# First mixture feed-forward of a two-layer decoder: the gate's exponential on GpSimd, the pads of the third value tile inside the second attention, four down products in a row

## The chip, the cores and the metric

One core of a Trainium2 chip runs the whole program; the other cores are idle. The metric is the device time of one execution in microseconds (us). Three executions of the kernel before give the times below, and a further one was recorded by the profiler. The engines are TensorE (PE, matmuls; "PEld" is its weight load), VectorE (DVE), ScalarE (ACT), GpSimd (POOL) and SyncE (SP), which issues most DMAs here. Each engine works through its own list of instructions in order and waits on semaphores for the others.

## The reference

Eight sequences of 128 tokens with 128 features pass through two decoder layers. Every sublayer is followed by `layernorm(x + sublayer(x))`. The order is self-attention, cross-attention to a context of 77 tokens, mixture feed-forward, then in the second layer a routed attention/state-space block, masked cross-attention and a second mixture. What matters here is the mixture of the first layer, which follows the first cross-attention:

```python
def _L0_ffn_ref(x, gate_w, down_w, down_b, up_w, up_b):     # x: 8 x 128 x 128
    TOP_K = 2
    pooled = x.mean(axis=1)
    gate = jax.nn.softmax(pooled @ gate_w.T, axis=-1)        # 8 sequences x 8 experts
    top_w, top_i = jax.lax.top_k(gate, TOP_K)
    top_w = top_w / (top_w.sum(axis=-1, keepdims=True) + 1e-08)
    ...
    h = jax.nn.gelu(jnp.einsum('bsd,bkcd->bksc', x, Wd) + bd[:, :, None, :], approximate=False)
    h = h * top_w[:, :, None, None]
    out = jnp.einsum('bksc,bkdc->bsd', h, Wu)
    out = out + (top_w[:, :, None] * bu).sum(axis=1)[:, None, :]
    return out
```

The gate weights belong to a whole sequence (the mean over its tokens), not to a token.

## The kernel before

The program is written by hand, engine by engine, in one block per engine. All activations stay on chip; the eight sequences are handled as two halves of four (HB = 4), so a half fills one PSUM bank of 128 x 512 float32. PSUM's eight banks are shared out by two rings. A product takes the next bank of its ring, and the engine that reads the bank gives it back: ScalarE empties the ring of banks 0 to 3, VectorE that of banks 4 to 7. The lists `ACT_JOBS` and `DVE_JOBS` (L162 to L169) fix the order of the jobs in each ring.

**Attention.** The three attentions share their code (`attention_tensor` L1406, `attention_scalar` L630, `attention_vector` L938, `attention_pool` L497). They are pipelined over the batch: in turn i VectorE takes the maxima of the scores of batch i + 2 (L945), the normalised output of batch i - 1 (L976, L988), the residual sum of batch i - 3 (L967) with its statistics (L1003 to L1005), and, for batch i - 4, the normalised result X (L997). Between the statistics and L997 GpSimd raises the variance to the power -0.5 (L501), one column for each batch. Hooks called `between` put other work into the last turns. For attention 2 these are the transposes of half 0 (`second_half`, L1583), then the four hidden products of half 0 with the pooling of batches 4 to 6 (`first_hidden`, L1579).

**The mixture.** All eight experts are computed for all tokens, and the weights of those not chosen are zero. Hidden units of two experts lie in one tile of 128, so there are four tiles t = 0 to 3. `hidden(c, ts)` (L1565) makes the down products of half c: it waits until ScalarE has copied the transposed half `x2T.c` to SBUF, and issues a matmul 128 x 512 for every tile. A float32 matmul stands in the trace as two instructions. ScalarE turns each into `hid` with the exact Gelu (`activated`, L708). `pool_tokens` (L1570) sums the tokens of a sequence by a matmul with a column of ones. VectorE copies the sums (L1098), PE makes the 8 x 8 logits (`logits8`, L1593), VectorE subtracts the maximum (L1100, L1102: g8) and ranks the experts by pairwise comparison (L1107 to L1111). In parallel ScalarE makes e8 = exp(g8) (L719), for which it calls for the table of the exponential first (L717) and needs the one of Gelu again after it. The `table` helper runs a dummy activation on one column to place the load. From e8 and the ranks VectorE makes the weights c8 (L1113 to L1119). PE spreads c8 over partitions (L1607, L1610), VectorE copies the result (L1120, L1121) and scales `hid` with it (L1127). PE adds the residual (L1600, a product with the identity), the weighted bias (L1616) and the up products (L1622) in one bank for each half; VectorE takes the statistics from there (L1140).

PE's order from the end of attention 2 is this: pooling of batch 7 (L1590), transposes of half 1, logits, residual of half 0, two hidden products of half 1, the spreading of c8, residual of half 1, the other two hidden products of half 1, then bias and up products of half 0 and of half 1.

**GpSimd** runs the eight powers of attention 2 with nothing between them. Then it fills the pads of V5, the value tile of the third attention: `value_ones(V5[:])` (L558) writes zeros into the 24 unused columns of every head (L482, 77 x 3072), waits for that, and writes the column of ones (L485). After it come the column mask (L559, L560), which is used much later for the values of the routed attention (L577), the fill of one stripe of `att` (L565), which waits until attention 2 has done its last product with the values, and the powers of the next norm (L571). Before attention 2 the same GpSimd code fills the pads of V1 and V2.

Of the kernel before, what the change touches and what calls it, by code (L numbers as in the profile page):

```python
# [23 lines left out]
ALU = mybir.AluOpType  # L24
ACT = mybir.ActivationFunctionType
AX = mybir.AxisListType

B, T, D = 8, 128, 128
H, HD = 16, 8
G = 4  # L30
J = H // G
# [146 lines left out]
def _build(nc, ctx, a, out):  # L178
    def sb(name, shape, dt=F32):
        return ctx.enter_context(nc.sbuf_tensor(name, shape, dt))  # L180

    def sem(name):
        return ctx.enter_context(nc.semaphore(name))
# [10 lines left out]
    colmask = sb("colmask", [128, J, D])  # L194
# [70 lines left out]
    dring = Ring([4, 5, 6, 7], sem("dve_bank_full"), sem("dve_bank_copied"), DVE_JOBS)  # L265
# [4 lines left out]
    def event(name):  # L270

        if name not in ev:
            ev[name] = sem(name)
        return ev[name]

    at1 = Attention(sem, "at1", T, 1 / math.sqrt(HD), kM1, V1, Wo1[:], XB, X[1])
    at2 = Attention(sem, "at2", NC, math.sqrt(HD), kM2, V2, Wp2[:], XB, X[0])
# [125 lines left out]
    dpos = qc  # L403

    hid = big[:, 0:4 * B * T].rearrange("p (t n) -> p t n", t=4)
    pooledT = sb("pooledT", [128, B]); ones_col = sb("ones_col", [128, 1]); e8 = sb("e8", [8, 8]); s8 = sb("s8", [8, 1])
    g8 = sb("g8", [8, 8]); m8 = sb("m8", [8, 1]); c8 = sb("c8", [8, 8]); t64 = sb("t64", [8, 8, 8]); e64 = sb("e64", [8, 8, 8])
    r8 = sb("r8", [8, 8]); cT = sb("cT", [128, 8]); cexp = sb("cexp", [128, 4, B])

# [37 lines left out]
    def _(pool):  # L447
        P_ = nc.gpsimd

        def step(ins):  # L450

            pool.wait_ge(pool_step.sem, pool_step.then(ins))

        def affine(t, op, pattern, multiplier=1):
            return P_.affine_select(out=t, in_=t, compare_op=op, fill=1.0, base=0, pattern=pattern,
                                    channel_multiplier=multiplier)
# [6 lines left out]
        P_.memset(onesb[:], 1.0)  # L463
        P_.memset(zerob[:], 0.0)
        P_.memset(ones_col[:], 1.0)
        P_.memset(upb3[:], 0.0).then_inc(event("upb_zero"), 1)
        step(P_.memset(eps_col[:], EPS))
        affine(ident[:], ALU.not_equal, [[-1, 128]]).then_inc(const_ready, 1)
# [10 lines left out]
        def value_ones(*values):  # L479

            for v in values:
                ins = P_.memset(v[:, :, :, HD:VW], 0.0)  # L482
            step(ins)
            for v in values:
                ins = P_.memset(v[:, :, :, HD:HD + 1], 1.0)  # L485
            ins.then_inc(event("v_ones"), 1)
# [10 lines left out]
        def attention_pool(at, later=None):  # L497

            for b in range(B):
                pool.wait_ge(at.eps_ready, b + 1)  # L500
                P_.tensor_tensor(out=rstd[:, b:b + 1], in0=ve[:, b:b + 1], in1=neg_half[:, 0:1], op=ALU.pow)\  # L501
                    .then_inc(at.rstd_ready, 1)
                if later:
                    later()

        def wide(bias):
# [7 lines left out]
                         in1=ident[0:E0, 0:E0].rearrange("p (e o) -> p e o", o=1).to_broadcast([E0, E0, BN]), op=ALU.mult)  # L514
# [25 lines left out]
        def residual2():  # L540

            loaded(pool, "l2")
            P_.tensor_tensor(out=XB[:], in0=X[1][:], in1=wide(bp2), op=ALU.add).then_inc(at2.xb_ready, 1)
# [3 lines left out]
        for _ in range(3):  # L547
# [5 lines left out]
        P_.tensor_tensor(out=sq[:, 0:HB], in0=qc[:, 0:HB], in1=qc[:, 0:HB], op=ALU.mult).then_inc(event("q_sq"), 1)  # L553
        pool.wait_ge(at1.x_ready, B)
        residual2()
        attention_pool(at2)

        value_ones(V5[:])  # L558
        step(P_.memset(colmask[:], 0.0))  # L559
        affine(colmask[:].rearrange("p j (g i d) -> p j g i d", g=G, i=J), ALU.not_equal, [[1, J], [0, G], [-1, J], [0, HD]], 0)\  # L560
            .then_inc(event("colmask"), 1)

        pool.wait_ge(event("colmask"), 1)
        pool.wait_ge(at2.pv_done, B)
        P_.memset(att[32:64, 0:W768], 1.0).then_inc(event("proj_ones"), 1)  # L565
        pool.wait_ge(event("proj_ones"), 1)
# [35 lines left out]
    def _(act):  # L602
        A_ = nc.scalar.activation
# [5 lines left out]
        def copy_out(name, dst, view, func=ACT.Identity, **kw):  # L609

            A_(dst, view(aring.take(act, name)), func, **kw).then_inc(aring.copied, 1)
# [50 lines left out]
        def table(func):  # L662

            k = next(tables)
            A_(table_out[:, k:k + 1], eps_col[:], func)
# [48 lines left out]


        copy_out("x2T.1", half(xT, 1), bank4)
        table(ACT.Exp)  # L717
        dring.wait_copied(act, "logits8")
        A_(e8[:], g8[:], ACT.Exp).then_inc(event("gate3_exp"), 1)  # L719
        activated(1)  # L720


# [637 lines left out]
    def _(pe):  # L1360
# [204 lines left out]
        def hidden(c, ts):  # L1565
            aring.wait_copied(pe, f"x2T.{c}")
            for t in ts:
                product(aring, f"hid.{t}.{c}", down3T[:, t * 128:(t + 1) * 128], half(xT, c))
# [28 lines left out]
        def residual(c):  # L1597

            ups.append(fill(dring, f"up.{c}"))
            M_(PS[:, ups[c], :], ident[:], flat(half(X[0], c)), start=True, stop=False)  # L1600

        residual(0)
        hidden(1, (0, 1))
        pe.wait_ge(event("c8_ready"), 1)
        for e in range(E0):

# [2 lines left out]
        ins.then_inc(dring.full, 1)  # L1609
        nc.tensor.transpose(PS[0:8, cT_bank, 0:8], c8[:], ident[0:8, 0:8]).then_inc(dring.full, 1)  # L1610
        residual(1)
        hidden(1, (2, 3))
        dring.wait_copied(pe, "cT")
        for c in range(2):
            for b4 in range(HB):
# [36 lines left out]
        i = fill(dring, "scol")  # L1652
# [6 lines left out]
        i = fill(dring, "rank")  # L1659
# [5 lines left out]
        i = fill(dring, "cumU")  # L1665
# [53 lines left out]
        for e in range(2):  # L1719
            if e:  # L1720
                pe.wait_ge(event("sa_ready"), 1)
            for n in range(2):
                for c in range(4):
                    for a in range(2):
                        g = 2 * e + a
# [125 lines left out]
        for c in range(2):  # L1851
            i = fill(dring, f"dposA.{c}")
# [5 lines left out]
        for c in range(2):  # L1858
            if c:
                pe.wait_ge(event("chosen_copied"), 7 + NH)  # L1860
            i = fill(dring, f"dposS.{c}")
# [7 lines left out]
        for c in range(2):  # L1869
            dring.wait_copied(pe, f"dposS.{c}")  # L1870
            i = fill(dring, f"dl.{c}")
# [90 lines left out]
```

## Time and profile before

| | |
|---|---|
| median of 3 runs | 438.21 us (437.77 to 443.17) |
| profiled execution | 440.69 us in all, span 438.9 us |
| mean granted clock of PE | 0.984 |
| PE busy | 391.8 us (89%), 4048 instructions |
| PE weight loads busy | 263.1 us (60%) |
| VectorE busy | 288.7 us (66%) |
| ScalarE busy | 232.3 us (53%) |
| GpSimd busy | 131.4 us (30%), 122 instructions |
| chain that ended last, by engine | PE 70%, VectorE 13%, ScalarE 10%, issue 4%, DMA 1%, GpSimd 1% |

The span is the time from the first to the last instruction on the core; the execution's time holds some start and end beside it. The chain follows back from the last instruction, at each step to what released it or to the instruction before it on its engine. "Issue" is time in which an engine waited for nothing that the profile shows. The granted clock of PE is 1.00 at 2.4 GHz and 0.50 at 1.2 GHz. PE is busy in nine tenths of the span, so the time is set by PE's work and by the places where PE waits.

### The profile page before, as it was taken

How to read it: one execution, taken by the hardware profiler on the slowest of the kernel's cores; microseconds unless marked ns; L12 is line 12 of the kernel's file. 1: busy time of each engine (PE TensorE's matmuls, PEld its weight loads, DVE VectorE, ACT ScalarE, POOL GpSimd, SP SyncE). 2: the span in 40 equal slices, each digit the busy share in tenths (PEclk: the TensorE clock that was granted, in tenths of full speed). 3: DMA queues.
4: the chain of work that ended last, by engine and by line, in shares of the span. 5: the costliest groups of instructions: out<-in, count | busy, mean ns of one | idle time of the engine just before them, and what ended most of it. 6: DMA issues, size and time to landing. Idle time of an engine off the chain costs nothing.

```text
span 438.9 us, 10077 instructions
## 1 busy us (share of the span) xinstructions
PE 391.8 (89%) x4048; PEld 263.1 (60%) x4059; DVE 288.7 (66%) x715; ACT 232.3 (53%) x431; POOL 131.4 (30%) x122
## 2 busy tenths in 40 slices
PE   3688998988998999996899999988999899999992
PEld 2445666546775674664677766835677466666662
DVE  5786885845656677677799798643566644544556
ACT  1234656536675537789999996025556352222220
POOL 5838645300016041000799797010010100000001
PEclk9899999999999899998999999999999999999998
DMA  7320000000000000030223320090000000000001
GB/s 182 67 44 3 3 2 4 1 1 3 3 3 1 1 0 1 1 114 0 73 82 99 109 75 34 12 277 1 3 3 4 1 0 0 1 1 1 0 0 48
DMA packets 16881, 13.84 MB, mean 32 GB/s; under 512 B 6548, under 2 KB 14133, under 8 KB 16837
## 3 DMA queue, kind: packets, MB, share of 16 engines
q1 hardware_dynamic: 15538, 12.51, 9.9%
q10 hardware_dynamic: 1299, 0.71, 0.5%
q8 instruction: 32, 0.52, 0.5%
q14 instruction: 12, 0.10, 0.1%
HBM read 12.64 MB, written 0.57 MB: 30 GB/s over the span
## 4 chain that ended last, share of the span: by engine, by line
PE 70%; DVE 13%; ACT 10%; issue 4%; DMA 1%; POOL 1%; ACTq 0%; POOLq 0%; DVEq 0%
PE PS L1810 9%; PE PS L1889 6%; PE PS L1893 6%; PE PS L1443 6%; PE PS L1920 6%; PE PS L1389 5%; PE PS L1797 4%; PE PS L1422 4%; ACT att L638 4%; PE PS L1460 3%; PE PS L1375 3%; PE PS L1507 2%; ACT outT L649 2%; PE PS L1622 2%; DVE XH L908 2%
## 5 line engine op out<-in xcount | busy, mean ns | idle before, releaser
L638 ACT ACTIVATE att<-PS 77x512 f32<-77x512 f32 (+1 forms) x96 | 51.7, 591 | 45.9 <-PE PS L1446 45.9
L945 DVE TENSOR_REDUCE mxp<-PS 128x4 f32<-128x308 f32 (+1 forms) x96 | 48.0, 536 | 32.1 <-PE PS L1422 32.1
L501 POOL TENSOR_TENSOR rstd<-ve,neg_half 128x1 f32<-128x1 f32 x24 | 13.3, 553 | 117.9 <-DVE ve L1005 117.9
L871 ACT ACTIVATE kM<-PS 128x512 f32<-128x512 f32 x32 | 19.1, 597 | 55.5 <-PE PS L1889 55.5
L1262 DVE TENSOR_TENSOR_SCAN big<-big,PS 128x768 f32<-128x768 f32 x22 | 38.1, 1743 | 3.4 <-PE PS L1797 3.3
L1328 DVE TENSOR_TENSOR big<-kM,PS 128x512 f32<-128x512 f32 x32 | 21.9, 687 | 27.3 <-PE PS L1893 26.0
L495 POOL TENSOR_TENSOR rstd<-ve,neg_half 128x4 f32<-128x4 f32 x6 | 6.2, 1030 | 104.7 <-DVE ve L901 104.7
L1889 PE MATMUL PS<-xT,V 128*128 128x512 f32 x64 | 33.0, 596 | 1.1 <-DVE xT L1316 0.8
L1893 PE MATMUL PS<-xT,V 128*128 128x512 f32 x64 | 32.7, 592 | 0.0
L1920 PEld LDWEIGHTS PS<-big 128*128 128x128 f32 x256 | 29.7, 192 | 3.4 <-issue 3.4
L1920 PE MATMUL PS<-big 128*128 128x128 f32 x256 | 29.7, 275 | 0.0
L1375 PE MATMUL PS<-negsel,identb 128*128 128x512 bf16 x108 | 26.3, 379 | 3.8 <-DVE big L1043 1.9
L531 POOL TENSOR_TENSOR hr<-hvar,half_bh 77x8 f32<-77x8 f32 (+1 forms) x7 | 22.8, 3266 | 9.4 <-DVE hvar L928 9.4
L824 ACT ACTIVATE att<-big,BT 128x256 f32<-128x256 f32 x58 | 24.7, 501 | 0.0
L1446 PE MATMUL PS<-flipped,negsel 32*77 32x128 bf16 (+1 forms) x384 | 24.6, 215 | 0.0
L1349 DVE SCALAR_TENSOR_TENSOR R<-PS,aff,R 128x128 f32<-128x128 f32 x56 | 15.8, 344 | 11.2 <-PE PS L1920 11.2
L1443 PE MATMUL PS<-qT,kM 32*77 32x128 f32 x512 | 21.0, 276 | 1.8 <-ACT att L638 1.1
L654 ACT ACTIVATE flipped<-PS 128x128 f32<-128x128 f32 (+1 forms) x33 | 10.7, 325 | 21.0 <-PE PS L1475 15.8
L1893 PEld LDWEIGHTS PS<-xT,V 128*128 128x128 f32 x64 | 12.2, 190 | 15.3 <-issue 14.8
L1375 PEld LDWEIGHTS PS<-negsel,identb 128*128 128x128 bf16 x118 | 10.7, 98 | 16.9 <-issue 3.3
L1797 PE MATMUL PS<-ident,att 128*128 128x128 f32 x128 | 19.3, 273 | 1.5 <-ACT att L824 1.2
L1262 DVE TENSOR_TENSOR_SCAN untransposed<-untransposed,PS 128x768 f32<-128x768 f32 x10 | 17.5, 1748 | 4.4 <-PE PS L1797 4.2
(369 smaller groups left out, 909.7 us busy)
## 6 DMA issues: line engine op xcount, KB each, us to landing
kM<-Cdram SPq DMA_DIRECT2D x6, 384.0 KB, 3.5
XH<-Cdram SPq DMA_DIRECT2D x5, 384.0 KB, 3.5
xT<-Cdram SPq DMA_DIRECT2D x5, 384.0 KB, 3.5
V<-in_L_ffn_Wg SPq DMA_DIRECT2D x1, 1024.0 KB, 5.4
V<-in_L_ffn_Wu SPq DMA_DIRECT2D x1, 1024.0 KB, 8.0
out_x<-X SPq DMA_DIRECT2D x2, 256.0 KB, 2.3
ctxN<-in_ctx ACTq DMA_DIRECT2D x1, 308.0 KB
X<-in_x ACTq DMA_DIRECT2D x1, 256.0 KB, 4.0
```

The costliest lines, as they stand in the source:

```text
L638: A_(PT[0:nk, i % 2, g], bank4(at.bank("exp", i, g), nk), ACT.Exp, scale=at.scale)\
L824: ins = A_(scaled[s % 2][k], duT[:, k, :], ACT.Identity, scale=BT[:, k, s:s + 1])
L945: V_.tensor_reduce(mxp[:, b % 3, g, 0:J], PS[:, at.bank("max", b, g), 0:J * nk].rearrange("p (j k) -> p j k", j=J), axis=AX.X, op=ALU.max) ...
L1262: V_.tensor_tensor_scan(hst[m % NHS], dA[m % NDA], dBu[m % NDB], 0.0, ALU.mult, ALU.add)\
L1375: M_(PS[:, bank, :], identb[:], negsel[:].rearrange("p j t -> p (j t)"), start=True, stop=True)
L1443: M_(PS[0:nk, at.bank("exp", b, g), j * T:(j + 1) * T], at.kM[rows(g), j, b, :], qT[rows(g), b, :], start=not at.masked, stop=False)
L1446: ins = M_(PS[0:nk, at.bank("exp", b, g), j * T:(j + 1) * T], negsel[rows(g), j, 0:nk], upper(flipped)[rows(g), (b - 1) % 2, 0:T], start=F ...
L1797: ins = nc.tensor.transpose(dBu[n % NDB][:, 128 * k:128 * (k + 1)], scaled[s % 2][k][:, 128 * h:128 * (h + 1)], ident[:])
L1810: ins = M_(y_piece(h, lo, hi), ident[:], hC[n % NHC][:, lo:hi], start=False, stop=(n // NH == DS - 1 and (h, lo) != (0, 512)))
L1889: M_(PS[:, n % 2, :], Wg6[:, e, i * 128:(i + 1) * 128], half(xT, c), start=True, stop=True)\
L1893: M_(PS[:, 2 + n % 2, :], Wu6[:, e, i * 128:(i + 1) * 128], half(xT, c), start=True, stop=True)\
L1920: ins = M_(PS[:, 4 + (2 * e + c) % 4, b4 * D:(b4 + 1) * D], hidE[e % 2][:, i, b * T:(b + 1) * T], Wd6[:, NI * e + i, :], start=(i == 0), s ...
```

## The change

It has three parts.

1. **The exponential.** GpSimd gets a constant tile `base8` of 8 x 8, filled with the number e at the start. After the eight powers of attention 2 it waits for g8 and computes e8 = base8 to the power g8. ScalarE's table call, its wait and its exponential go away; ScalarE stays with the table of Gelu from half 0 to half 1. The event `gate3_exp`, on which VectorE waits at L1112, is now sent by GpSimd. The event `colmask` is replaced by GpSimd's own step counter.
2. **The pads.** The filling of V5 follows the power of batch 0 in attention 2, the column mask that of batch 1, through the hook `later` of `attention_pool`, which attention 1 uses already for other powers.
3. **PE's order.** The four hidden products of half 1 stand in a row ahead of the residual of half 0; the residual of half 1 keeps its place behind the spreading of c8.

```diff
@@ -403,7 +403,7 @@
-    pooledT = sb("pooledT", [128, B]); ones_col = sb("ones_col", [128, 1]); e8 = sb("e8", [8, 8]); s8 = sb("s8", [8, 1])
+    pooledT = sb("pooledT", [128, B]); ones_col = sb("ones_col", [128, 1]); e8 = sb("e8", [8, 8]); base8 = sb("base8", [8, 8]); s8 = sb("s8", [8, 1])
@@ -463,6 +463,7 @@
         P_.memset(ones_col[:], 1.0)
+        P_.memset(base8[:], math.e)
         P_.memset(upb3[:], 0.0).then_inc(event("upb_zero"), 1)
@@ -553,14 +554,18 @@
         residual2()
-        attention_pool(at2)
-
-        value_ones(V5[:])
-        step(P_.memset(colmask[:], 0.0))
-        affine(colmask[:].rearrange("p j (g i d) -> p j g i d", g=G, i=J), ALU.not_equal, [[1, J], [0, G], [-1, J], [0, HD]], 0)\
-            .then_inc(event("colmask"), 1)
-
-        pool.wait_ge(event("colmask"), 1)
+
+        def column_mask():
+
+            step(P_.memset(colmask[:], 0.0))
+            step(affine(colmask[:].rearrange("p j (g i d) -> p j g i d", g=G, i=J), ALU.not_equal,
+                        [[1, J], [0, G], [-1, J], [0, HD]], 0))
+
+        steps = iter([lambda: value_ones(V5[:]), column_mask])
+        attention_pool(at2, lambda: next(steps, lambda: None)())
+
+        pool.wait_ge(dring.copied, dring.index["logits8"] + 1)
+        P_.tensor_tensor(out=e8[:], in0=base8[:], in1=g8[:], op=ALU.pow).then_inc(event("gate3_exp"), 1)
         pool.wait_ge(at2.pv_done, B)
         P_.memset(att[32:64, 0:W768], 1.0).then_inc(event("proj_ones"), 1)
@@ -714,9 +719,6 @@
         copy_out("x2T.1", half(xT, 1), bank4)
-        table(ACT.Exp)
-        dring.wait_copied(act, "logits8")
-        A_(e8[:], g8[:], ACT.Exp).then_inc(event("gate3_exp"), 1)
         activated(1)
@@ -1599,8 +1601,8 @@
+        hidden(1, range(4))
         residual(0)
-        hidden(1, (0, 1))
         pe.wait_ge(event("c8_ready"), 1)
@@ -1609,7 +1611,6 @@
         residual(1)
-        hidden(1, (2, 3))
         dring.wait_copied(pe, "cT")
```

## Rows read from the trace of the kernel before

**Rows 1.** The page's head: length of the profiled execution
```profile
span 438.9 us, 10077 instructions
```

**Rows 2.** Chain that ended last, 137 to 150: start us, us, engine line
```profile
137.80 2.65 DVE X L997
...
141.56 2.01 PE PS L1600 x2
143.57 2.43 PE PS L1389 x4
...
147.71 1.72 PE PS L1389 x4
149.43 0.89 PE PS L1616 x8
```

**Rows 3.** Timeline, end of attention 2: start us, us, engine, line, operation [idle before]
```profile
137.70 2.65 POOL L482 MEMSET V<- 77x3072 f32 x1
...
137.80 2.63 DVE L997 TENSOR_SCALAR X<-R,mv,rstd 128x128 f32<-128x128 f32 x1 [0.66 <-POOL rstd L501]
...
140.58 0.35 PE L1575 MATMUL PS<-ones_col,X 128*128 128x1 f32 x2 [1.60 <-DVE X L997]
...
141.47 0.60 ACT L611 ACTIVATE xT<-PS 128x512 f32<-128x512 f32 x1 [2.32 <-PE PS L1384]
```

**Rows 4.** L997, every instruction: ns min/median/max, first and last start
```profile
L997 DVE TENSOR_SCALAR X<-R,mv,rstd x24: 334/341/2634, 59.6 to 346.4; 128x128 f32<-128x128 f32 x24
```

**Rows 5.** Windows: us, busy of PE, PEld, DVE, ACT, POOL; then granted clock, DMA
```profile
138.40:141.40 3.00, 1.40 (x15) 1.17 (x13) 2.20 (x2) 0.69 (x1) 2.79 (x4) 1.00 0.00 0
141.40:146.00 4.60, 4.60 (x11) 1.83 (x12) 2.44 (x13) 4.15 (x6) 1.78 (x2) 0.63 0.00 0
```

**Rows 6.** Timeline of the gate, 141 to 147
```profile
141.31 1.15 POOL L455 TENSOR_SCALAR_AFFINE_SELECT colmask<-colmask 128x512 f32<-128x512 f32 x1
...
141.79 0.21 DVE L1102 TENSOR_SCALAR g<-PS,m 8x8 f32<-8x8 f32 x1
142.04 0.41 DVE L1107 TENSOR_TENSOR t<-g 8x64 f32<-8x64 f32 x1
...
142.51 0.73 POOL L565 MEMSET att<- 32x768 f32 x1
...
142.62 0.21 DVE L1109 TENSOR_TENSOR e<-e,earlier 8x64 f32<-8x64 f32 x1
...
143.71 0.15 DVE L1113 TENSOR_REDUCE s<-e 8x1 f32<-8x8 f32 x1 [0.40 <-ACT e L719]
144.52 0.22 DVE L1119 TENSOR_SCALAR c<-c,m 8x8 f32<-8x8 f32 x1
...
146.89 4.91 DVE L1127 TENSOR_TENSOR big<-big,cexp 128x512 f32<-128x512 f32 x8
```

**Rows 7.** GpSimd's groups by form: count | busy us, mean ns | idle before
```profile
L531 POOL TENSOR_TENSOR hr<-hvar,half_bh 77x32 f32<-77x32 f32 x3 | 16.2, 5428 | 9.4 <-DVE hvar L928 9.4
L531 POOL TENSOR_TENSOR hr<-hvar,half_bh 77x8 f32<-77x8 f32 x4 | 6.6, 1645 | 0.0
```

**Rows 8.** L955, every instruction: ns min/median/max
```profile
L955 DVE TENSOR_TENSOR mxp<-mxp x48: 165/175/177, 30.4 to 332.3; 128x16 f32<-128x16 f32 x48
```

**Rows 9.** Timeline inside attention 2, around the first batch's power
```profile
116.11 0.55 POOL L501 TENSOR_TENSOR rstd<-ve,neg_half 128x1 f32<-128x1 f32 x1 [30.26 <-DVE ve L1005]
...
117.12 0.29 DVE L967 TENSOR_TENSOR R<-XB,PS 128x128 f32<-128x128 f32 x1 [1.09 <-ACT flipped L654]
...
119.63 0.34 DVE L997 TENSOR_SCALAR X<-R,mv,rstd 128x128 f32<-128x128 f32 x1
```

**Rows 10.** Timeline of PE in and before the scan, two pauses
```profile
199.27 1.32 PE L1822 MATMUL PS<-ident,untransposed 128*128 128x128 f32 x6 [2.08 <-ACT V L804]
...
208.62 0.66 PE L1797 MATMUL PS<-ident,qT 128*128 128x128 f32 x4 [1.56 <-ACT att L824]
```

**Rows 11.** Waits of PE, start of the kernel: us in total, times, longest
```profile
PE PS L1384 <- DMA ctxN<-in_ctx: 7.0, 1, 7.0
```
## The prediction

> **What bounds the kernel now.** I read four views. First the page and its windows: the profiled execution spans 438.9 us [rows 1], TensorE (PE) is the busiest engine, and the change touches only the passage from the end of attention 2 to the down products of the mixture, 137 to 150 us. Then the chain of work that ended last in that passage: what ends last there is all that can move the time. It runs X (L997, VectorE), pooling and transposes, the residual product of half 0 (L1600), hidden products of half 1 (L1389), the gate's matmuls, the residual of half 1 and two more hidden products, then the up products from L1616 on, at 149.43 [rows 2]. Neither ScalarE nor GpSimd is on it. Last the timelines, for what stands behind each piece, and the windows for the clock.
>
> The reader is to see three things. (1) The chain's step of 2.65 us at L997 is one small instruction: the 24 L997s take 341 ns at the median and one takes 2634 [rows 4]. That one starts at 137.80, 0.10 behind GpSimd's fill of V5's pads (2.65 us from 137.70), and ends when the fill does, 140.43 against 140.35 [rows 3]. PE waits 1.60 us for it [rows 3]. (2) Until 141.40 the granted clock is 1.00 of 2.4 GHz; in 141.40 to 146.00 it is 0.63 on average, a mixture of 1.2 and 2.4 GHz, right behind that pause [rows 5]. The residual product and two hidden products, six matmuls of 512 columns, take 2.01 + 2.43 = 4.44 us on the chain; at full clock four such take 1.72, so 0.43 each [rows 2]. (3) The sum s8 starts at 143.71, behind ScalarE's exponential [rows 6], but c8 is ready at 144.52 + 0.22 = 144.74, while PE works on hidden products until 146.00 [rows 2, 6]. So the exponential has 1.26 us of cover, and taking it from ScalarE returns nothing in itself.
>
> **The change, part by part.**
>
> *Pads of V5 and the column mask into attention 2.* The fill now follows the first batch's power, which ends at 116.11 + 0.55 = 116.66, so it lies in about 116.6 to 119.3, with the ones (0.3 or so more) to 119.6. The next L997 starts at 119.63 [rows 9], so it is clear by a hair, and a miss would hold it only for the rest of the small fill. Before it VectorE runs maxima and other operations that read PSUM; the trace shows no fill beside those shapes, which I bound below. In the old place the stalled L997 falls back from 2.63 to 0.34 us. PE reaches the last pooling matmul without its 1.60 us: it is still pooling batches 4 to 6 until then. Term: -1.60.
>
> *Row of four hidden products before the residual.* The work is the same, the order is not. Before, the residual product (it needs only half 0) ran while ScalarE copied x2T.1; now the hidden products come first and PE waits for that copy. All moves 1.60 forward: the gate's logits end at 141.56 - 1.60 = 139.96; the copy ran 141.47 to 142.07 [rows 3], so now 139.87 to 140.47, and the first product can start at about 140.52, a term of +0.56. ScalarE is free for the copy: its last activation of half 0 is over when the transposes are.
>
> *The clock.* The pause of 1.60 is gone, and what is left is a pause of 0.56. Elsewhere a pause of 1.56 us left the clock at 1.00, one of 2.08 came ahead of a fall [rows 10]. I take it that the clock stays at 2.4 GHz: six matmuls at 0.43 are 2.58 instead of 4.44, term -1.86. From the windows: 4.60 x (1 - 0.63) = 1.70 [rows 5]; bounds 0 (it falls anyway) and 1.86.
>
> *GpSimd's power.* Removed from ScalarE: two table loads, the dummy and the 8 x 8 exponential, all off the chain. Added: one power of 8 x 8 on GpSimd. The nearest row is 77 x 8, 1.65 us; the upper bound is 77 x 32, 5.43 [rows 7]; I take 1.65, since eight columns are what both have. g8 is ready at 142.00 before [rows 6], 140.40 after; the power ends at about 142.1; from s8 to c8 took 144.74 - 143.71 = 1.03, so c8 at 143.2. PE gets to the gate's matmuls at 140.52 + 8 x 0.43 (four hidden products) + 0.86 (residual) = 144.8. Cover left 1.6, cost nothing. Behind the power on GpSimd stand only the fill of att and the powers of the next norm, which wait for the up products anyway. The new 8 x 8 fill of base8 at the start costs less than the 0.73 of a 32 x 768 one [rows 6], under PE's wait of 7.0 for the context's load [rows 11]: nothing. No DMA is added or moved.
>
> *Behind it.* From 146.00 to 149.43 the chain holds the gate's matmuls, the second residual and two hidden products of 1.72 [rows 2]. The hidden ones are gone from there, 3.43 - 1.72 = 1.71 stay, and L1616 starts at 144.8 + 1.71 = 146.5 against 149.43: -2.9. Term by term: -1.60 + 0.56 - 1.86 = **-2.90**. VectorE's scaling began 0.89 behind 146.00 and took 4.91 for eight tiles [rows 6]; now it begins at 145.7 and the first tile is there at 146.3, before PE's bias matmuls end (146.5 + 0.89), and each further one takes it 0.61 against PE's 0.89 for eight such matmuls. What follows waits on this chain, so the gain passes to the end: span 438.9 - 2.9 = 436.0. The profiled execution took 440.69 in all, 1.8 beyond its span; the median of the runs is 438.21 (437.77 to 443.17), so I subtract there: 438.2 - 2.9 = **435.3 us**.
>
> **Where a rule weighs in.** L1107 took 0.41 us where L1109, same shape, took 0.21, and it ended at 142.45, when GpSimd's affine_select (141.31 + 1.15) did [rows 6]; L1109 ran beside the fill of att untouched. The Trainium skill ("SBUF — State Buffer", "Who interferes with whom") says that a VectorE instruction with two SBUF inputs contends with a GpSimd one that reads SBUF, not with one that only writes it. By that rule the new power would hold L1107 to L1110. For the power the trace speaks against it: L955, which reads two SBUF operands, has 177 ns as its longest of 48 [rows 8], some of them beside the powers of 5.43 us.
>
> **Rivals.**
>
> *A. The clock falls all the same* (or falls in the scan stage, where the shifted pauses of 2.08 and 1.56 us lie [rows 10]). For: pooling matmuls of one column and transposes are thin work around the 0.56 pause. Against: 1.56 passed unharmed. Gain 2.90 - 1.70 = 1.2, 437.0. 0.15.
>
> *B. The unprofiled runs of before have no such clock fall*, so it cannot be returned: -1.60 + 0.56 = -1.04, 437.2. The profiled run is 2.5 over the median, which allows it. 0.10.
>
> *C. The fill holds VectorE in its new place.* L967 at 117.12 would wait to about 119.25: 2.1 us in an iteration in which VectorE has 1.09 of idle time before L967 [rows 9]. At worst all 2.1 come back: 435.3 + 2.1 = 437.4. Against: in 141 to 142.5 VectorE's reads of PSUM beside GpSimd's work took 0.21 at most [rows 6]. 0.07.
>
> *D, the other side. The power is slow and c8 late.* Nothing on the page shows a power with other exponents than -0.5. It is free up to 144.8 - 1.03 - 140.4 = 3.4 us. At the 5.43 of 77 x 32, c8 comes at 146.9, PE waits 2.1, a pause like the 2.08 that preceded a fall, so 1.70 more: +3.8 - 2.9 = +0.9, 439.1. It is slower than before once PE waits over 2.9, or over 1.2 with the fall: powers over 4.6. If the power also holds VectorE's ranking, 1.28 us of it (142.04 to 143.32) comes behind the power instead of beside it, and the free limit falls to 2.1, still over 1.65. 0.05.
>
> *E. The fall before the scan vanishes too*, as its place shifts: 1.7 more, 433.6. 0.08.
>
> *F. The forecast*, 0.55; its own range is 434.6 to 436.2 (the copy's wait and the clock's bound by either view, and the runs' usual scatter).
>
> **The numbers.** The range leaves out D and little else: 433.5 to 437.9. Every case lies within 2% (8.8 us, about what a measurement of this kernel can tell from no change), so same 0.96, and 0.02 for each side for a change of the clock's course elsewhere.
>
> **What would show it.** L997 of batch 7 at 0.34 us and PE's pause ahead of L1575 gone. V5's fill at 116.6 with L967 and the maxima beside it unstretched. Granted clock 1.00 from 138 to 150. Power near 1.65 us, with c8 ready before PE ends the residual of half 0. No table load between x2T.1 and hid.0.1. L1616 some 8.7 us behind the last L997's start instead of 11.6. A stretched maximum, a granted 0.5 behind the logits, or PE waiting at L1607 would prove the sum wrong at that term.

## The result and the profile after

| | before | after |
|---|---|---|
| median, 20 executions each | 439.38 us (437.05 to 443.17) | 436.94 us (435.12 to 440.76) |
| ratio to before | 1 | 0.9939, 95% interval 0.9913 to 0.9964 |
| profiled execution | 440.69 us, span 438.9 | 435.12 us, span 433.3 |
| mean granted clock, profiled | 0.984 | 0.991 |
| PE busy | 391.8 us | 388.6 us |
| VectorE busy | 288.7 us | 286.1 us |
| ScalarE busy | 232.3 us | 229.1 us |
| GpSimd busy | 131.4 us | 133.2 us |

The change makes the kernel 0.6% faster, 2.4 us by the medians and 1.6 to 3.8 by the interval; the forecast was 2.9 us and 435.3. One execution in all, of start_alone at 446.82 us with a mean clock of 0.936, is left out of its ratio but not of its median. The two profiled executions differ by more, 5.6 us of span, and three places make that up. The changed kernel lacks a stretch of low clock near 19 us that the other execution had (its last X of attention 2 starts at 135.88 instead of 137.80 [rows 3], 1.92 earlier, with the same work before it). That 1.92 is not the change's: the wait of PE for XH between 14 and 18 us, which the change leaves alone, was 2.0 to 3.5 us long in all eleven profiles with the old start, and a low stretch followed it in seven and not in four. The passage of the change gives 2.60. The other 1.08 come later, where each has one fall of the clock, at 199.5 in before and at 186.5 in the changed kernel, beside the one in the last 10 us that every profile has.

I measure the **passage** in PE's timeline, from the start of the hidden products of half 0 to the start of the first bias matmul. It is 14.45 us before (134.82 to 149.27) and 11.85 after (132.90 to 144.75). Single profiles can be compared on it, because the work ahead of it repeats: from the first batch's power of attention 2 to the start of the passage took 18.71 or 18.72 us in the profile of before, of after and of every experiment that left this stretch alone. Its first and last group, before and after:

```profile
134.82 3.60 PE L1389 MATMUL PS<-xT,down3T 128*128 128x512 f32 x8
149.27 1.05 PE L1616 MATMUL PS<-upb,cT 128*128 128x128 f32 x8
```

```profile
132.90 3.60 PE L1391 MATMUL PS<-xT,down3T 128*128 128x512 f32 x8
144.75 1.05 PE L1617 MATMUL PS<-upb,cT 128*128 128x128 f32 x8
```

First the chain that ended last in the profile after (start us, us, engine and line, in the changed file's lines), to be read against [rows 2]:

```profile
136.50 0.79 PE PS L1577 x8
137.28 0.51 PE PS L1386 x4
...
137.82 0.61 ACT xT L616
138.42 0.24 issue
138.66 3.67 PE PS L1391 x8
142.34 0.86 PE PS L1602 x2
...
143.86 1.05 PE PS L1602 x2
144.91 0.89 PE PS L1617 x8
```

L997 is off the chain. Where it took 2.65 us, PE now goes from pooling (L1577) to the transposes without a pause. New on the chain is ScalarE's copy of x2T.1, 0.61, with 0.24 until PE's first product runs. The four hidden products and the residual take 4.5 us together.

Then the timeline of GpSimd and VectorE at the fill's new place in attention 2, against [rows 9]:

```profile
114.68 2.66 POOL L483 MEMSET V<- 77x3072 f32 x1
117.40 0.32 POOL L486 MEMSET V<- 77x128 f32 x1
...
115.20 0.29 DVE L969 TENSOR_TENSOR R<-XB,PS 128x128 f32<-128x128 f32 x1 [1.09 <-ACT flipped L659]
115.43 0.48 DVE L947 TENSOR_REDUCE mxp<-PS 128x4 f32<-128x308 f32 x1
...
117.62 0.18 DVE L957 TENSOR_TENSOR mxp<-mxp 128x16 f32<-128x16 f32 x1
117.71 0.34 DVE L999 TENSOR_SCALAR X<-R,mv,rstd 128x128 f32<-128x128 f32 x1
```

The fill of 2.66 us covers the residual sum L969 and four maxima (L947), and they have their old lengths (0.29 as in [rows 9]; the maxima 0.42 to 0.48, and the longest of all 96 is 692 ns in both kernels). X of batch 0 starts at 117.71 and takes 0.34, 0.01 ahead of the end of the small fill at 117.72. X in all its 24 instructions, against [rows 4]:

```profile
L999 DVE TENSOR_SCALAR X<-R,mv,rstd x24: 336/341/349, 57.7 to 340.8; 128x128 f32<-128x128 f32 x24
```

Last the gate, in the timeline, against [rows 6], and the windows of [rows 5]:

```profile
135.88 0.35 DVE L999 TENSOR_SCALAR X<-R,mv,rstd 128x128 f32<-128x128 f32 x1 [0.66 <-POOL rstd L502]
...
138.43 1.68 POOL L568 TENSOR_TENSOR e<-base,g 8x8 f32<-8x8 f32 x1 [2.58 <-DVE g L1104]
138.53 0.21 DVE L1110 TENSOR_TENSOR e<-g 8x64 f32<-8x64 f32 x1
...
140.14 0.15 DVE L1115 TENSOR_REDUCE s<-e 8x1 f32<-8x8 f32 x1 [0.67 <-POOL e L568]
...
140.95 0.22 DVE L1121 TENSOR_SCALAR c<-c,m 8x8 f32<-8x8 f32 x1
```

```profile
138.40:141.40 3.00, 2.74 (x7) 1.33 (x8) 1.86 (x11) 1.39 (x3) 2.41 (x2) 1.00 0.00 0
141.40:146.00 4.60, 4.60 (x36) 2.84 (x35) 2.16 (x6) 2.86 (x4) 0.00 (x0) 1.00 0.00 0
```

The power took 1.68 us (1.65 forecast from [rows 7]); e8 to c8 took 1.03; c8 was there at 141.17, PE asked for it at 143.1. L1110, the second operation of the ranking, began inside the power and took 0.21; the first (L1109 here, L1107 before) took 0.21 too, though it began 0.05 ahead of the power, and not the 0.41 of L1107 beside the column mask [rows 6]. The granted clock is 1.00 where it was 0.63 [rows 5].

### The profile page after: what moved, and what is told of

Its sections match the earlier page's. It is cut to its first block, busy times and chain, and to the rows that moved or that the text cites. A ratio compares the mean times of both kernels' runs of the same rounds, so it can differ in the third digit from the quotient of the medians.

```text
span 433.3 us, 10074 instructions
## 1 busy us (share of the span) xinstructions
PE 388.6 (90%) x4048; PEld 261.9 (60%) x4059; DVE 286.1 (66%) x715; ACT 229.1 (53%) x427; POOL 133.2 (31%) x124
## 4 chain that ended last, share of the span: by engine, by line
PE 70%; DVE 12%; ACT 11%; issue 4%; DMA 1%; POOL 1%; ACTq 0%; POOLq 0%; DVEq 0%
PE PS L1811 9%; PE PS L1890 6%; PE PS L1894 6%; PE PS L1445 6%; PE PS L1921 6%; PE PS L1391 5%; PE PS L1798 4%; PE PS L1424 4%; ACT att L643 4%; PE PS L1462 3%; PE PS L1377 3%; PE PS L1509 2%; ACT outT L654 2%; PE PS L1623 2%; DVE XH L910 2%
## 5 line engine op out<-in xcount | busy, mean ns | idle before, releaser
L947 DVE TENSOR_REDUCE mxp<-PS 128x4 f32<-128x308 f32 (+1 forms) x96 | 48.0, 536 | 31.9 <-PE PS L1424 31.9
L659 ACT ACTIVATE flipped<-PS 128x128 f32<-128x128 f32 (+1 forms) x33 | 10.7, 325 | 20.7 <-PE PS L1477 15.5
```

The source lines that it names most:

```text
L947: V_.tensor_reduce(mxp[:, b % 3, g, 0:J], PS[:, at.bank("max", b, g), 0:J * nk].rearrange("p (j k) -> p j k", j=J), axis=AX.X, op=ALU.max) ...
```

## The experiments

Those with a median (6 to 12 executions, the whole change 20) have their ratio to runs of the kernel before on the same chip; the others have one profiled execution, and are read by the passage.

| kernel | passage | median, ratio to before (95% interval) |
|---|---|---|
| before | 14.45 | |
| whole change | 11.85 | 436.94, 0.9939 (0.9913 to 0.9964) |
| pads_only | 11.58 | 436.94, 0.9939 (0.9916 to 0.9961) |
| pads_back | 16.47 | 441.78, 1.0051 (1.0018 to 1.0084) |
| act_exp | 11.85 | |
| old_order | 11.67 | |
| late_fill | 14.05 | |
| kept_busy | 13.31 | |
| res_first | 11.06 | 436.77, 0.9912 (0.9876 to 0.9948) |
| fill_twice | 11.85 | |
| pow_late | 14.43 | |
| start_fill | 11.06 | 433.49, 0.9853 (0.9803 to 0.9902) |
| start_alone | 14.49 | 435.91, 0.9914 (0.9887 to 0.9941) |

### The parts one by one

**pads_only**: the kernel before with the second part of the change alone (and the wait for g8 ahead of att's fill, without the power).

```diff
-        attention_pool(at2)
-        value_ones(V5[:])
...
+        steps = iter([lambda: value_ones(V5[:]), column_mask])
+        attention_pool(at2, lambda: next(steps, lambda: None)())
+        pool.wait_ge(dring.copied, dring.index["logits8"] + 1)
         pool.wait_ge(at2.pv_done, B)
```

> The kernel before with the pads and the column mask moved into attention 2, nothing else; the exponential stays on ScalarE, PE's order stays. I measure the passage from the start of the hidden products of half 0 to the start of the first bias matmul in the timeline of PE: 14.45 us before, 11.85 with the whole change. Theory (the stalled X and the clock fall behind it are the whole gain): the last X takes 0.34, PE's pause of 1.60 is gone, the clock stays at 1.00, and the residual product now fills the wait for the copy of x2T.1. What is new is that c8 becomes late: copy, table load 1.28, dummy and exponential follow one another on ScalarE, so c8 comes about 0.6 after PE's two hidden products. Passage 11.8, so as good as the whole change, and about 2.5 us faster than before. Rival (the new order or the power has a share of its own): 12.4 or more.

The passage is 11.58 and the ratio 0.9939, the same as with the whole change. PE's timeline:

```profile
139.64 1.12 PE L1603 MATMUL PS<-X,ident 128*128 128x512 f32 x2
140.60 1.88 PE L1392 MATMUL PS<-xT,down3T 128*128 128x512 f32 x4
142.93 0.63 PE L1610 MATMUL PS<-ident,c 8*64 8x8 f32 x16 [0.46 <-DVE c L1122]
...
146.27 1.05 PE L1619 MATMUL PS<-upb,cT 128*128 128x128 f32 x8
```

The residual (L1603) follows the logits without a gap, the two hidden products follow it, and PE waits 0.46 for c8. So moving the pads and the mask is the whole gain; the power and the order add nothing to it, and by the passage take 0.27 back.

**pads_back**: the whole change without its second part; the power then stands behind the column mask.

> The whole change, but the fill of V5 and the column mask back behind the eight powers of attention 2 (and then the power of the gate behind them). Theory: X of the last batch is held for 2.3 us again, PE pauses 1.6, the clock falls to 0.5 in most executions, and the order with the hidden products first adds its wait for the copy; the power starts behind the column mask. Passage 14.5 to 15.5 us against 14.45 before and 11.85 with the whole change; time as before or up to 1 us slower. Rival (order and power give a part of the gain): passage 13.5 or less, time faster than before by 1 us.

Slower than before by 0.5%. PE's timeline, and the window behind the logits (span, busy of the engines, granted clock):

```profile
140.56 0.35 PE L1575 MATMUL PS<-ones_col,X 128*128 128x1 f32 x2 [1.61 <-DVE X L997]
...
142.37 6.48 PE L1389 MATMUL PS<-xT,down3T 128*128 128x512 f32 x8 [0.75 <-ACT xT L614]
...
141.40:148.00 6.60, 5.85 (x10) 2.60 (x10) 2.34 (x13) 2.11 (x4) 3.39 (x3) 0.50 0.00 0
```

The pause of 1.6 is back, the wait for the copy (0.75) comes right behind it, and the clock is at 0.5 for the whole of 141.40 to 148.00. The eight hidden instructions run at 1.2 GHz until 148.0, 0.85 ahead of their end, and take 6.48 us instead of 3.67. I had the direction, not the size: 16.47 against the 14.5 to 15.5 expected, because I let the clock come back as early as it did before (by 145.0). In time it is 2.4 us slower by the medians, where I had allowed 1. Without the pads, order and power are a loss.

**act_exp**: the whole change with the exponential on ScalarE again.

```diff
         pool.wait_ge(dring.copied, dring.index["logits8"] + 1)
-        P_.tensor_tensor(out=e8[:], in0=base8[:], in1=g8[:], op=ALU.pow).then_inc(event("gate3_exp"), 1)
...
+        table(ACT.Exp)
+        dring.wait_copied(act, "logits8")
+        A_(e8[:], g8[:], ACT.Exp).then_inc(event("gate3_exp"), 1)
```

> The whole change, but the gate's exponential on ScalarE with its two table loads as before; GpSimd waits for g8 all the same ahead of its fill. Theory (the exponential is covered either way): e8 comes within 0.3 us of the power's, c8 long before PE has ended its five products; the activations of half 1 start about 1.5 us later, and no one waits for them. Passage 11.85, the same as with the power. Rival (freeing ScalarE of two table loads of 1.28 is part of the gain): passage 12.9 to 14.4.

11.85 to the hundredth. From the end of g8 to the start of s8 it was 1.72 us here and 1.79 with the power. The activations of half 1 started at 143.06, 2.7 us behind the first product's start instead of 1.1, and nothing waited for them. Moving the exponential to GpSimd is worth nothing in this order.

**old_order**: the whole change with PE's old order, so pads and power.

> The whole change, but PE's order as before: residual of half 0, two hidden products, the gate's matmuls, residual of half 1, two more. It is pads_only with the power on GpSimd in place of the exponential on ScalarE. Theory (power and exponential with its tables take the same time from g8 to c8, 2.82 against 2.75): PE waits 0.5 to 0.6 us for c8, passage 11.65, 0.07 over pads_only and 0.2 under the whole change. Rival (the power frees ScalarE, which then serves PE sooner): 11.1, as with the residual first and all four in a row.

11.67, PE waiting 0.55 for c8: as theory had it (11.65), and 0.18 under the whole change. With a power as with an exponential, the old order pays about 0.5 at c8, the new order 0.75 at the copy.

### What held VectorE

**late_fill**: the kernel before, the fill in the same stage but behind the last X.

```diff
         attention_pool(at2)
+        pool.wait_ge(at2.x_ready, B)
         value_ones(V5[:])
```

> The kernel before with one wait more: GpSimd starts the fill of V5's pads only when the last X of attention 2 is written. Same work, same engine, same stage, order and exponential as before. Theory (what costs is that the fill starts just ahead of an instruction that reads and writes SBUF alone): the last X takes 0.34 us, PE's pause is gone, copies from PSUM and 8 x 64 operations beside the fill are not held; passage 11.8 to 12.5, the upper end if the small operation c8 is held by the column mask or the fill of att. Rival (any fill of GpSimd's in this stage slows VectorE, so that it must leave the stage): the copy of the pooled sums or g8 is held until the fill ends, passage 13.5 or more.

Timeline of GpSimd, VectorE and PE:

```profile
137.90 2.65 POOL L482 MEMSET V<- 77x3072 f32 x1 [0.44 <-DVE X L998]
...
141.51 1.15 POOL L455 TENSOR_SCALAR_AFFINE_SELECT colmask<-colmask 128x512 f32<-128x512 f32 x1 [0.15 <-POOL colmask L560]
...
137.50 0.35 DVE L998 TENSOR_SCALAR X<-R,mv,rstd 128x128 f32<-128x128 f32 x1 [0.66 <-POOL rstd L501]
...
138.94 0.17 DVE L1099 COPY pooledT<-PS 128x8 f32<-128x8 f32 x1 [1.09 <-PE PS L1576]
...
141.75 0.84 DVE L1116 SCALAR_TENSOR_TENSOR c<-r,e 8x8 f32<-8x8 f32 x1
...
143.52 0.63 PE L1608 MATMUL PS<-ident,c 8*64 8x8 f32 x16 [1.23 <-DVE c L1120]
```

The last X takes 0.35, and the copy of the pooled sums from PSUM takes 0.17 in the middle of the fill of 137.90 to 140.55. That is the theory's part, and the stall of 2.3 us is gone without the fill leaving the stage. But the passage is 14.05, above the 11.8 to 12.5 of the theory and where the rival's number lay, though not by the rival's cause: the later column mask (affine_select, 141.51 to 142.66) now meets c8's first operation, which reads two tiles of SBUF (L1116, 8 x 8). It takes 0.84 instead of 0.14 and ends as the mask does. PE waits 1.23 for c8, and the clock falls at 144.6. Against pads_only the way from the residual to the spreading of c8 is 0.78 longer, and from there to the bias matmuls 1.70, the clock's part. The chain of the gate has as little room as the last X had.

**fill_twice**: the whole change, the fill of zeros done twice in its new place.

```diff
-        steps = iter([lambda: value_ones(V5[:]), column_mask])
+        def pads_twice():
+
+            step(P_.memset(V5[:][:, :, :, HD:VW], 0.0))
+            value_ones(V5[:])
+
+        steps = iter([pads_twice, column_mask])
```

> The whole change, with the zeros of V5's pads written twice in the new place, so that the fill reaches over the first batch's X in attention 2. The stretch from the first batch's power to the first hidden product of half 0 takes 18.71 us in the kernel before and in every kernel so far. Theory (the new place is free only because the fill ends 0.03 us ahead of X of batch 0): operations that read PSUM beside the fill stay at their length, X of batch 0 is held for about 2.7 us, from 0.34 to about 3.0, the next turn's residual sum and maxima come behind it, and the stretch grows by 1 to 2 us, to 19.7 to 20.7. Rival (attention has room for it): X is held, the stretch stays within 0.3 of 18.71. Third possibility, the maxima are stretched as well: stretch above 21.

Timeline of GpSimd and VectorE in attention 2:

```profile
116.42 2.66 POOL L566 MEMSET V<- 77x3072 f32 x1
119.14 2.66 POOL L483 MEMSET V<- 77x3072 f32 x1
...
118.48 0.85 DVE L952 TENSOR_REDUCE mxp<-PS 128x4 f32<-128x308 f32 x2
119.37 0.17 DVE L962 TENSOR_TENSOR mxp<-mxp 128x16 f32<-128x16 f32 x1
119.46 2.42 DVE L1004 TENSOR_SCALAR X<-R,mv,rstd 128x128 f32<-128x128 f32 x1
119.72 2.16 DVE L962 TENSOR_TENSOR mxp<-mxp 128x16 f32<-128x16 f32 x1
119.80 2.08 DVE L1010 BATCH_NORM_STATS2 st<-R 128x6 f32<-128x128 f32 x1
```

The maxima beside the fills keep their length (0.85 for two). L1004, X of batch 0, starts at 119.46, takes 2.42 and ends with the second fill, 121.88 against 121.80. L962 and L1010 behind it are in the queue and show 2.1 us each, though alone they take 0.17 and 0.28. The stretch from the first power to the passage grew from 18.71 to 20.18, inside the 19.7 to 20.7 expected. X was to be held for 2.7 us and lost 2.1 (2.42 less 0.34). So the change's place for the fill is free by its timing and not by its nature: 2.1 us of hold cost 1.5 us there.

These rows agree with a rule of the Trainium skill ("SBUF — State Buffer", "Who interferes with whom"): VectorE in a 2-port mode, which by the page copies and tensor_scalar can enter, contends with GpSimd; operations with two SBUF inputs contend with a GpSimd instruction that reads SBUF, not with one that only writes it. X (tensor_scalar, SBUF to SBUF) was held by fills, L1116 and L1107 (two SBUF inputs) by the column mask, while the ranking's first two operations ran inside late_fill's fill at 0.21 each; reads of PSUM were held by neither. On the power the measurement decides: it reads two tiles of SBUF, and did not hold such operations (next run).

### What the clock gives

**kept_busy**: the kernel before, the pause filled with seven idle matmuls (the trace has six of them).

```diff
+        keep_busy(5, 7)
         pool_tokens(7, B)
```

> The kernel before with seven idle matmuls of 512 columns (into a free PSUM bank) ahead of the last pooling matmul, to fill the pause of 1.60 in which PE waits for the stalled X. The stall itself stays. This takes the clock's share alone. Theory (the fall is due to the pause): granted clock 1.00 from 138 to 150; residual and two hidden products take 2.6 instead of 4.4, but then PE waits about 0.5 for c8, which comes where it did; passage 14.45 - 1.86 + 0.6 = 13.2. Rival (the clock falls for the thin work in general, or independent of the pause): passage 14.4, granted 0.5 behind the logits.

PE's timeline:

```profile
138.92 1.46 PE L1375 MATMUL PS<-negsel,identb 128*128 128x512 bf16 x6
140.45 0.35 PE L1575 MATMUL PS<-ones_col,X 128*128 128x1 f32 x2
...
144.66 0.63 PE L1608 MATMUL PS<-ident,c 8*64 8x8 f32 x16 [0.46 <-DVE c L1119]
...
148.00 1.05 PE L1617 MATMUL PS<-upb,cT 128*128 128x128 f32 x8
```

One of its windows (span, busy of the engines, granted clock), where before has 0.50:

```profile
142.50:143.00 0.50, 0.50 (x2) 0.20 (x2) 0.43 (x3) 0.50 (x1) 0.50 (x1) 1.00 0.00 0
```

X is held as before (2.63), the granted clock is 1.00 in the passage and until 189 us, and the passage is 13.31, against 13.2 expected. So the fall of the clock behind the pause is worth 14.45 - 13.31 = 1.14 us in the kernel before. It lies wholly between the residual and the spreading of c8: 4.44 us before, 3.30 here, of which 2.84 are matmuls and 0.46 is PE's wait for c8. So the matmuls are 1.60 faster, and 0.46 of that is waited for c8. What is left to the whole change, 13.31 - 11.85 = 1.46, is the stall (1.73 up to the logits) and the wait at c8 (0.46), less the new wait for the copy (0.75). That is one execution with the pause filled; the three profiles with the pause empty (before, pads_back, start_alone) all show the fall.

The timed executions fit this. Each lists its mean granted clock, and these come in steps of 0.004. Means of the time, with the number of executions (those of before are the 57 timed beside the experiments):

| mean clock | before | whole change |
|---|---|---|
| 0.992 | 437.5 (9) | 435.5 (9) |
| 0.988 | 438.5 (20) | 437.1 (4) |
| 0.984 | 440.2 (17) | 438.5 (6) |
| 0.980 | 441.5 (6) | 440.8 (1) |
| 0.976 | 443.2 (5) | none |

At equal clock the changed kernel is 1.4 to 1.9 us faster in the rows with four executions or more, about the 1.46 of the passage. The rest of the 2.4 is that it is in the top row more often, 9 of 20 against 9 of 57. Where a timed execution has its low stretches isn't recorded, so this can't say how many of them had the fall in the passage. In the profiles they lie near 19, in the passage, at 186 to 203, at 282 to 295 and in the last 10 us, and which of them a profile has differs.

### The power's cover

**pow_late**: the whole change with a second power ahead of the gate's.

```diff
         pool.wait_ge(dring.copied, dring.index["logits8"] + 1)
+        step(P_.tensor_tensor(out=hr1[0:NC, 0:22], in0=hvar[0:NC, 0:22], in1=half_bh[0:NC, 0:22], op=ALU.pow))
         P_.tensor_tensor(out=e8[:], in0=base8[:], in1=g8[:], op=ALU.pow).then_inc(event("gate3_exp"), 1)
```

> The whole change with a second power (77 x 22, result not used) on GpSimd between the arrival of g8 and the gate's power, about 3.8 us, so that the two take the 5.4 of rival D. It tests the cover that the prediction gave the power. Theory (the power is free up to about 3.4 us): c8 comes at g8 + 5.5 + 1.05, 2.0 us after PE has ended its five products; passage 11.85 + 2.0 = 13.8 with the clock at 1.00, and up to 1.5 more if the clock falls behind the pause; VectorE's ranking beside the first power stays at 0.21 for each operation. Rival (GpSimd holds VectorE's ranking, which reads two SBUF operands, until its power is over): the ranking's first operation is stretched to the power's end, c8 1.3 us later still, passage 15.1 or more.

Timeline of VectorE, GpSimd and PE:

```profile
139.05 0.24 DVE L1111 TENSOR_TENSOR e<-g 8x64 f32<-8x64 f32 x1
...
138.96 3.89 POOL L568 TENSOR_TENSOR hr<-hvar,half_bh 77x22 f32<-77x22 f32 x1 [2.59 <-DVE g L1105]
142.93 1.63 POOL L569 TENSOR_TENSOR e<-base,g 8x8 f32<-8x8 f32 x1
...
145.67 0.63 PE L1610 MATMUL PS<-ident,c 8*64 8x8 f32 x16 [1.96 <-DVE c L1122]
```

PE waited 1.96 (2.0 expected), the clock fell behind it (0.50 from 147.0), and the passage is 14.43, between the two values given. The low stretch lasts until 150.2, past the passage's end at 147.85, so the passage holds only a part of its price. Of the ranking's operations the second began inside the power of 3.89 us and took 0.24, and the next two 0.21 each: the power does not hold VectorE. Powers of GpSimd measured here: 0.55 us for 1 column, 1.68 for 8, 3.89 for 22, and 5.43 for 32 [rows 7]; 8 columns cost the same on 8 partitions (1.68) as on 77 (1.65).

### Two versions beyond the change

**res_first**: the residual ahead of the four hidden products.

```diff
-        hidden(1, range(4))
         residual(0)
+        hidden(1, range(4))
```

> The whole change with one line of PE's order moved: the residual of half 0 stands ahead of the four hidden products instead of behind them, so it fills PE's wait for the copy of x2T.1 (0.75 us in the changed kernel). Theory: nothing else is near the chain there (c8 is ready 2 us before PE asks for it), so the passage shrinks by the wait: 11.85 - 0.75 = 11.1. Time about 0.7 us below the changed kernel's, 436.2, near the limit of what can be told. Rival (the wait comes back at c8, as in pads_only, where PE waited 0.46 for it): 11.5 or more.

The passage is 11.06. The residual ran from 138.05 and the first hidden product followed at 139.01 with no wait; c8 was ready at 141.38, PE came at 142.53. Against the changed kernel that is 0.79 less, the wait of 0.75 and a little. In time (436.77) it can't be told from the whole change. Here the four in a row do pay, 0.61 against old_order, which differs in nothing else, since they cover c8 while the residual covers the copy.

**start_fill**: res_first, and the fills at the start behind XH.

```diff
         P_.tensor_tensor(out=spread8[:].rearrange("p (e c) -> p e c", e=E0), in0=spread8[:].rearrange("p (e c) -> p e c", e=E0),
...
+        pool.wait_ge(event("xh1"), 2)
         value_ones(V1)
```

> res_first and one wait more: at the start of the kernel GpSimd begins the fills of the pads of V1 and V2 (2.65 and 2.70 us, at 11.76 and 14.67 in the changed kernel) only when both halves of XH are written. There the eight operations L910 (128 x 128, SBUF to SBUF) take 8.19 us and PE waits 2.78 to 3.39 for them. Theory (the same stall as that of the last X of attention 2): the second half of XH is ready at about 12.5, PE makes its transposes as soon as it is through with the context's keys and values (14.2 to 14.7), and the start is 2.7 to 3.3 us shorter, more where the clock fell behind the pause. Time 432.5 to 433.8. Rival (what follows is bound by VectorE's copies or by GpSimd's later squares and residual, which come 2 to 3 us later or at the same time as before): under 1 us.

The same stall stands at the start of the kernel before. The first view is of L908 in it (ns min/median/max), the next of L911, the same line, in start_fill, with GpSimd's first fill and PE's transposes:

```profile
L908 DVE TENSOR_SCALAR XH<-X,mv,rstd x8: 339/362/3718, 9.5 to 14.7; 128x128 f32<-128x128 f32 x8
```

```profile
L911 DVE TENSOR_SCALAR XH<-X,mv,rstd x8: 333/341/1124, 9.3 to 12.2; 128x128 f32<-128x128 f32 x8
...
12.54 2.68 POOL L483 MEMSET big<- 128x3072 f32 x1 [0.66 <-DVE XH L911]
...
14.11 1.04 PE L1387 MATMUL PS<-ident,XH 128*128 128x128 f32 x8
```

The longest of the eight falls from 3.72 to 1.12 us. What is left is not the fill's: that L911 starts at 10.85 and ends at 11.97, beside GpSimd's product L514 (10.86 to 11.89, two SBUF inputs), which lay ahead of the fills before too. The fill starts at 12.54 behind the last, and PE makes all transposes in one go at 14.11 instead of waiting 3.39 until 17.75. The first scores of attention 1 start at 21.19, against 23.43 in the changed kernel and 25.24 before. The median is 433.49, ratio 0.9853 (0.9803 to 0.9902), from six executions: the best version, 1.5% below before, and inside the 432.5 to 433.8 expected.

**start_alone**: the kernel before with only that wait.

> The kernel before with one wait more and nothing of the change: the fills of the pads of V1 and V2 at the start begin only when XH is written. start_fill had the same wait on top of res_first. Theory (the two stalls are the same mechanism in two places and their gains add): the first scores of attention 1 start at about 21.2 us as in start_fill (25.24 before, of it 1.7 for a clock fall behind the pause), the passage at the end of attention 2 stays at 14.45 with its stall of 2.63 us; time 2.5 to 4 us below before. Rival (the gain of start_fill was a lucky draw of the clock): within 1.5 us of before.

First scores at 21.09, passage 14.49 with X held for 2.63, median 435.91, ratio 0.9914, 3.8 us below before by the ratio. The two places are independent in the profiles: start_fill has the early scores (21.19) and the short passage (11.06) of res_first. In time their gains add as far as can be told: 0.9914 x 0.9912 (res_first) is 0.983, and start_fill gave 0.985, with 0.9803 to 0.9902 as its interval. One line at the start, without any of the change, gives about as much as the change (0.9887 to 0.9941 against 0.9913 to 0.9964).

## Why the prediction was right

The time fell inside the range and the mechanism is the forecast one. The time by itself, 436.94, lies nearer to what rivals A (437.0), B (437.2) and C (437.4) gave than to 435.3, since the level was set too low (the last step below). The gain tells them apart: 2.4 us (1.6 to 3.8) against 2.9 forecast and 1.2, 1.0 and 0.8 by the rivals, though B's, set right below, comes to 1.5, just outside the interval. So do the traces: a fall of the clock before, none after, and no held operation in attention 2. Step by step:

- **The stall, -1.60.** Shown. PE's pause is gone and the logits start 1.73 earlier in the passage (6.54 behind its start before, 4.81 after). pads_only has the gain alone, pads_back loses it, late_fill, with X at 0.35 and the logits at 4.81 too, shows that it is the meeting with X that costs and not the fill's stage.
- **The wait for the copy, +0.56.** It measured 0.75. The copy ended at 138.42 where a product was expected 0.05 later; PE took 0.24 until it ran. The term was mis-sized by that.
- **The clock, -1.86.** The six products' worth of work took 1.70 less, 0.16 short of the count; a further 0.08 was lost around them. Sum of the passage -1.73 + 0.75 - 1.70 + 0.08 = -2.60, against -2.9.
- **Rival B, no clock fall in before: -1.04.** This was the step with a flaw. I took 0.56 + (-1.60) and forgot that at full clock the kernel before would itself wait for c8. kept_busy shows that wait, 0.46, so the change is worth 1.46 there. All three profiles with the pause empty have the fall; whether timed executions without it are among those of before isn't shown.
- **The exponential, nothing.** Shown by act_exp. The cover of 1.26 us was there only because the matmuls behind the pause ran at half clock: with the clock at 1.00 and the old order it is a wait of 0.46 (kept_busy, pads_only). In the new order the cover is there, and the power's time was right, 1.65 forecast and 1.68 measured; its free limit of 3.4 us is borne out by pow_late, where 5.60 from first to last made PE wait 1.96, which puts it at 3.6.
- **The fill's new place, nothing.** Right, and as close as said: 0.01 us. fill_twice shows rival C's price with its mechanism corrected: not PSUM's readers are held but X and what is queued behind it.
- **The level, 435.3.** I subtracted from a median of three, 438.21; over 20 executions it was 439.38. Of the distance of 1.6 between 435.3 and 436.94, 1.2 are this, and the rest is that the gain was 2.4 and not 2.9.

What I did not see: that the change's other two parts were not needed, since pads_only gives the same time. The sum held them at nothing and at +0.56, and that should have been said as a comparison with the pads alone.

## What to carry to other kernels

Look in the view of a line (shortest, median, longest) for an instruction whose longest is many times its median; section 5 of the page has only the mean. Then look at what GpSimd did beside it: here an operation of 0.34 us within SBUF waited 2.3 us for a fill of pads that nobody needed yet. Put such fills where VectorE reads PSUM, behind the last small operation and not ahead of it, and test the room by doubling them. When PE's pause goes, price the next arrival on the chain at full clock before adding parts that are to hide it.

## What the runs showed of the hardware

- A held VectorE instruction does not show as idle time. It and those queued behind it show as busy and long (2.42, 2.16 and 2.08 us in fill_twice), so the wait views don't name GpSimd as the cause.
- A power on GpSimd, though it reads SBUF, let VectorE's two-input operations pass at 0.21 to 0.24 us, and one of 1.04 us at the start of the kernel before let L908 (tensor_scalar within SBUF) pass at 0.34; affine_select held them to its end (0.84 in late_fill, 0.41 in [rows 6]).
- A pause of 1.6 us of PE between thin work was followed by a granted 0.5 in before, pads_back and start_alone, one of 1.23 in late_fill and one of 1.96 in pow_late too; pauses of 0.46 to 0.75 in this stage were not (pads_only, old_order, the whole change, act_exp, fill_twice), nor was there a fall in res_first, without a pause. In pads_back, where a wait of 0.75 came behind the pause of 1.6, the low stretch was twice as long as in before (about 141 to 148 against 141 to 145).
- Between 14 and 18 us a longer pause did not always bring a fall: one was there in seven profiles (pauses of 1.96 to 3.48) and not in four (2.45 to 3.11, the changed kernel's 2.78 among them). The place of a fall is in part chance, and a single profile's time holds it.
